# Attention queries and keys in two float32r parts, 59 rows a head, a pair of heads on two row halves

## The chip, the cores and the metric

The kernel runs on one core of a Trainium2 chip. The metric is the time of one execution on the device in microseconds (us). Engines in the profile: PE is TensorE's matrix products, PEld its loads of the stationary operand, DVE VectorE, ACT ScalarE, POOL GpSimd, SP the engine that issues the transfers.

## The reference, cut to what matters

Input x is (1, 2048, 256) in float32. The model is feed-forward, attention, feed-forward, twice. The first pair of feed-forward layers has ternary weights and a silu gate, the second pair keeps 2 of each 4 hidden values. Both attentions are causal with 16 heads of 16:

```python
scores = einsum('bhqd,bhkd->bhqk', q, k) / sqrt(16)
# first attention: + slopes[h] * (k_pos - q_pos) for keys up to the query; second: q and k are rotated (RoPE)
scores = where(key > query, -inf, scores)
attn = softmax(scores, axis=-1)
y = einsum('bhqk,bhkd->bhqd', attn, v)
```

## The kernel before

The order of the phases is setup, feed-forward, qkv, attention, output projection, feed-forward, then the same again for the second layer. Each phase writes out one program per engine, and the engines meet at semaphores.

**qkv_phase** (L631) makes queries, keys and values for four blocks of 512 tokens. Each query or key element is split in three bf16 parts: ScalarE makes the first (L718), VectorE the remainder (L753), ScalarE the second (L706), GpSimd the third (L786). SP stores them to qk_scratch in DRAM (L825) and loads the keys back, head by head, to g.kt (L812): six sections of 16 rows (SROWS = 96, the products of parts in K_PARTS and Q_PARTS), three rows for the maxima, and in the first layer twelve for the ALiBi bias. So a head's contraction has 111 rows in the first layer and 99 in the second, and one head fills the array's rows.

**attention_phase** (L840) goes through 16 steps, one for each query block qb (0 to 3) and group hg of four heads; for qb from 1 the first two groups are a hardware loop (steps, L886). A step has 4(qb+1) key tiles of 128, called units u. In each unit TensorE makes the transposed scores of two pairs of heads (scores, L952, matmul at L964, with a mask product at L962 on the four diagonal units), ScalarE takes the exponential of two heads at once (L1118), and TensorE multiplies with the values of four heads, in float32, on four column tiles (values, L969, L980). These three are the step's places, three to a unit. PSUM banks 0 to 3 hold scores, 4 the output, 5 to 7 the products for the maxima.

The softmax needs each query's maximum before the step begins, so during a step TensorE also makes the products of queries and keys for the next step (max_product, L935, L948), 16(qb+1) items (head, query tile t, key block c), and VectorE reduces each (maxima, L1037): a plain reduction at L1049 for key blocks before the diagonal, a masked one at L1051 for the diagonal block, 128 to 512 wide. Item k uses bank 5 + (k+1) % 3 and waits for item k-3. The items are dealt over the places by max_done (L916); early_items (L913) says how many of the step after next are done at the end of a step. finish_maxima (L1054) negates and splits the maxima in three bf16 parts on VectorE, TensorE transposes them (L987) into bank 5, ScalarE copies them (L1109), and SP writes them as three rows of the queries (rows, L1143, L1146). The next step's scores wait for that transfer (cdma).

The waits on which the order of this work hangs are these:

```python
                if k >= 3:
                    e.wait_ge(s.mx, n + k - 2)            # L945, TensorE, before product k
...
                    if c < qb:
                        e.wait_ge(s.amm, n + k + 1 + (c == qb - 1))   # L1041, VectorE, before item k
```

## Time and profile before

| | us |
|---|---|
| median of the runs | 2012.33 (2009.31 to 2013.27, three runs) |
| profiled execution, span | 2008.3 |
| setup, 0 to 58 | 58 |
| first feed-forward, 58 to 194 | 136 |
| first qkv phase, 194 to 298 | 104 |
| first attention phase, 298 to 804 | 506 |
| first projection and second feed-forward, 804 to 972 | 168 |
| third feed-forward with its weights, 972 to 1162 | 190 |
| second qkv phase, 1162 to 1284 | 122 |
| second attention phase, 1284 to 1795 | 511 |
| second projection and fourth feed-forward, 1795 to 2008 | 213 |

How to read the rows below. A row of the windows has the stretch, its length, the busy time of each engine with the number of its instructions, TensorE's granted clock (1.00 is 2.4 GHz, 0.50 is 1.2 GHz), the share of time in which the DMA engines were busy, and GB/s. The windows of single steps begin and end where ScalarE ends its copy of a step's output (L1125). A row of the timeline has the start, the duration, engine, line, operation, output and inputs, how many instructions were merged, and in brackets how long the engine stood idle before it and who released it. TensorE's instructions overlap, so for them the distance between starts counts, not the duration.

### The profile page before, as it was taken

Reading aid. Unit: us, or ns where it says so; the run is one execution under the profiler, and the core shown is the slowest. Engines: PE = TensorE matmul, PEld = TensorE weight load, DVE = VectorE, ACT = ScalarE, POOL = GpSimd, SP = SyncE. Lnnn points to the kernel's source line nnn. Section 1 sums busy time; section 2 is a strip of 40 time slices with the busy share of each in tenths; the row PEclk is TensorE's granted clock in tenths of the full one; section 3 lists DMA queues with packets and bytes.
Section 4 is the critical chain, followed back from the end, with each engine's and each line's share of the span. In section 5 each row is a group of like instructions: output and inputs, shape, how many; then the busy total and the mean of one; then the engine's idle time right before and its main releaser. Section 6 shows DMA issues by size and latency. Waiting matters only on the chain. (4 is left out here: it accounts for less than half of the span.)

```text
span 2008.3 us, 29496 instructions
## 1 busy us (share of the span) xinstructions
PE 1627.6 (81%) x9772; PEld 913.3 (45%) x9772; DVE 1360.9 (68%) x3268; ACT 913.0 (45%) x1275; POOL 299.6 (15%) x227
## 2 busy tenths in 40 slices
PE   1687717898999999798599587279999999998896
PEld 0576613333333332687488466033333333336786
DVE  8664407778788881565599664277888888713897
ACT  3443404454655668244343222144565566661342
POOL 5332300000000000133043344000000000000243
PEclk9998858999999999899799788599999999998998
DMA  3001892111111000100100048711111110000000
GB/s 114 21 1 20 170 190 47 44 40 42 31 46 31 22 26 12 43 1 0 53 1 0 15 99 178 128 47 33 43 31 37 31 36 22 26 7 1 1 21 22
DMA packets 95600, 86.98 MB, mean 43 GB/s; under 512 B 6255, under 2 KB 92271, under 8 KB 93936
## 3 DMA queue, kind: packets, MB, share of 16 engines
q1 hardware_dynamic: 95490, 85.56, 18.2%
q8 instruction: 64, 1.05, 0.2%
q14 instruction: 46, 0.38, 0.1%
HBM read 62.07 MB, written 23.07 MB: 42 GB/s over the span
## 5 line engine op out<-in xcount | busy, mean ns | idle before, releaser
L1118 ACT ACTIVATE l_att_probs<-psum 128x1024 f32<-128x1024 f32 (+3 forms) x640 | 552.5, 892 | 341.9 <-PE psum L964 337.0
L1049 DVE TENSOR_REDUCE l_att_maxima<-psum 128x1 f32<-128x512 f32 x768 | 511.1, 687 | 140.9 <-PE psum L948 133.6
L948 PE MATMUL psum<-l_kt,l_att_qt 111*128 (+9 forms) x1280 | 416.2, 361 | 130.6 <-DMA l_att_qt<-in_qx_alibi 43.5
L964 PE MATMUL psum<-l_att_qt,l_kt 99*128 (+8 forms) x1280 | 354.1, 352 | 2.2 <-ACT l_att_probs L1118 1.3
L948 PEld LDWEIGHTS psum<-l_kt,l_att_qt 111*128 111x128 bf16 (+3 forms) x1280 | 117.5, 98 | 477.4 <-DVE l_att_maxima L1049 184.1
L980 PE MATMUL psum<-l_att_probs,l_att_vg 128*32 128x512 f32 (+3 forms) x2560 | 303.1, 546 | 5.7 <-ACT l_att_probs L1118 5.0
L1051 DVE CUSTOM_DVE_ANT_0 l_att_junk<-psum,consts 128x128 bf16<-128x128 f32 (+3 forms) x512 | 245.5, 481 | 0.0
L132 POOL TENSOR_TENSOR rstd<-var,mhalf 128x4 f32<-128x4 f32 x24 | 24.3, 1011 | 1285.8 <-DVE var L111 1285.8
L964 PEld LDWEIGHTS psum<-l_att_qt,l_kt 111*128 111x128 bf16 (+3 forms) x1280 | 118.4, 99 | 123.0 <-ACT l_att_probs L1118 37.5
L962 PE MATMUL psum<-later,identb 128*128 128x128 bf16 x512 | 105.3, 225 | 6.4 <-DMA l_att_qt<-l_att_ct 5.5
L980 PEld LDWEIGHTS psum<-l_att_probs,l_att_vg 128*32 128x32 f32 x2560 | 51.0, 108 | 98.0 <-issue 66.9
L1044 DVE COPY fence<-mhalf 128x1 f32<-128x1 f32 x128 | 19.2, 150 | 90.8 <-PE psum L948 90.5
L679 PE MATMUL psum<-l_qkv_xh,l_wqkv_h 128*128 128x512 f32 x96 | 46.5, 484 | 29.4 <-DVE l_qkv_xl L152 22.6
L1109 ACT ACTIVATE l_att_ct<-psum 12x512 bf16<-12x512 bf16 x32 | 18.5, 579 | 102.4 <-PE psum L987 102.1
L573 POOL TENSOR_TENSOR ffn1a_hl<-ffn1a_abs,ffn1a_hh 128x512 fp32r<-128x512 f32 x32 | 51.7, 1644 | 84.6 <-ACT ffn1a_hh L431 84.6
L573 POOL TENSOR_TENSOR ffn1b_hl<-ffn1b_abs,ffn1b_hh 128x512 fp32r<-128x512 f32 x32 | 51.7, 1644 | 84.6 <-ACT ffn1b_hh L431 84.6
L1076 DVE RECIPROCAL l_att_rinv<-psum 128x16 f32<-128x16 f32 x32 | 8.0, 251 | 80.8 <-PE psum L994 80.8
L962 PEld LDWEIGHTS psum<-later,identb 128*128 128x128 bf16 x512 | 50.4, 100 | 24.4 <-DMA l_att_qt<-l_att_ct 7.8
L354 PE MATMUL psum<-ffn0a_xh,w_ternary 128*128 128x512 f32 x128 | 53.5, 418 | 9.2 <-DVE ffn0a_h L478 7.8
L354 PE MATMUL psum<-ffn0b_xh,w_ternary 128*128 128x512 f32 x128 | 52.9, 413 | 9.2 <-DVE ffn0b_h L478 7.8
L354 PE MATMUL psum<-ffn1b_xh,wgu_h 128*128 128x512 f32 x128 | 51.3, 401 | 3.9 <-DVE ffn1b_xl L152 2.8
L354 PE MATMUL psum<-ffn1a_xh,wgu_h 128*128 128x512 f32 x128 | 51.3, 401 | 3.9 <-DVE ffn1a_xl L152 2.8
(200 smaller groups left out, 2998.4 us busy)
## 6 DMA issues: line engine op xcount, KB each, us to landing
l_att_vg<-v_scratch SPq DMA_DIRECT2D x80, 256.0 KB, 2.9
qk_scratch<-l_qkv_parts SPq DMA_DIRECT2D x32, 384.0 KB, 11.3
l_kt<-qk_scratch SPq DMA_DIRECT2D x48, 256.0 KB, 9.8
l_att_qt<-qk_scratch SPq DMA_DIRECT2D x156, 64.0 KB, 2.5
v_scratch<-l_qkv_vst SPq DMA_DIRECT2D x8, 1024.0 KB, 13.1
l_att_qt<-qk_scratch SPq DMA_DIRECT2D x12, 192.0 KB, 6.5
set_raw<-in_w_gu SPq DMA_DIRECT2D x2, 1024.0 KB, 6.5
x_resident<-in_x SPq DMA_DIRECT2D x1, 2048.0 KB, 15.5
```

The lines of the kernel that those rows point to most:

```text
L132: e.tensor_tensor(g.rstd[:, :], g.var[:, :], g.mhalf[:, :], ALU.pow).then_inc(s.rstd, 1)
L354: ins = e.matmul(g.ps[:, slots[c] + half, :], w_up[w][:, k, col:col + P], xp[x][:, k, :], start=k == 0 and q == 0, stop=k == KD - 1 and q ...
L573: e.tensor_tensor(hl[:, c // GCH, c % GCH, :], hs[:, c // GCH, c % GCH, :], hh[:, c // GCH, c % GCH, :].bitcast(F32), ALU.subtract).then_i ...
L679: ins = e.matmul(g.ps[:, bank, :], wq[w][:, k, col:col + P], xp[x][:, k, :], start=k == 0 and q == 0, stop=k == KD - 1 and q == len(terms) ...
L948: e.matmul(g.ps[:, 5 + (k + 1) % 3, 0:w], qt[:, ds(hg * HG + h, 1), t * P:(t + 1) * P].rearrange("p a t -> p (a t)"), g.kt[0:krows, ds(hg ...
L962: e.matmul(g.ps[:, h, off:off + P], g.identb[:, :], g.later[:, :], start=True, stop=False, skip_group_check=True)
L964: ins = e.matmul(g.ps[:, h, off:BLK], g.kt[0:krows, ds(hg * HG + h, 1), kt * P:(kt + 1) * P].rearrange("p a t -> p (a t)"), qt[:, ds(hg * ...
L980: ins = e.matmul(g.ps[h * VW:(h + 1) * VW, 4, off:BLK], vg[:, kt, h * VW:(h + 1) * VW], pr[:, u % 2, h, off:BLK], start=u == 0, stop=qb == ...
L1044: e.tensor_copy(g.fence[:, k % 4:k % 4 + 1], g.mhalf[:, 0:1])
L1049: e.tensor_reduce(dst, src, AX.X, ALU.max).then_inc(s.mx, 1)
L1051: e.tensor_tensor_reduce(out=junk[:, t, 0:w], in0=src, in1=mask[:, BLK - w:BLK], scale=1.0, scalar=NEG, op0=ALU.add, op1=ALU.max, accum_ou ...
L1118: e.activation(pr[:, u % 2, 2 * pair:2 * pair + 2, off:BLK], g.ps[:, 2 * pair:2 * pair + 2, off:BLK], ACT.Exp, scale=HD ** -0.5).then_inc( ...
```

## The change

Queries and keys are split in two float32r parts in place of three bf16 parts: ScalarE makes the first, VectorE the second, and GpSimd and ScalarE make no third and second part. Three sections of 16 rows remain; with three rows for the maxima and eight for the bias a head has 59 rows in the first layer and 51 in the second. Even heads lie in partitions 0 to 63, odd heads in 64 to 127 of the same tile (kt, qt: 8 pairs in place of 16 heads), so both are loaded by two transfers a section, and the row transfer of the maxima becomes two. The scratch in DRAM is float32. The mask product of 128 rows becomes two of 64 rows for each head. Products for the maxima come in pairs of heads, and the items, their shares (early_items, max_done, max_early) and both waits go by pairs. On VectorE the odd item of the block before the diagonal waits for the two diagonal products behind it, and for qb = 0 one wait and one fence stand before each pair. The loops over blocks and groups are written out. Setup copies the bias tables from DRAM to DRAM. The slots for the parts in the qkv phase are three, not four.

```diff
-SROWS = 6 * HD
-Q_PARTS = (0, 0, 1, 0, 2, 1)
-K_PARTS = (0, 1, 0, 2, 0, 1)
+NPAIR = HEADS // 2
+HALF = P // 2
+Q_PARTS = (0, 0, 1)
+K_PARTS = (0, 1, 0)
+SECS = len(Q_PARTS)
+XROW = 2 * HD
+MROWS = 3
...
+            for to, of in [("kx", "in_kx"), ("qx_alibi", "in_qx_alibi"), ("qx_rope", "in_qx_rope")]:
+                e.dma_start(a[to], a[of]).then_inc(s.xin, 16)
+            e.wait_ge(s.xin, 80)
...
-        parts = sb("parts", [P, NM, 3, BLK], BF16)
+        NS = 3
+        parts = sb("parts", [P, NS, 2, BLK], F32R)
...
-            def second_part(b, m):
-                e.wait_ge(s.r1, b * NM + m + 1)
-                e.activation(parts[:, m, 1, :], z[:, m, :], ACT.Copy).then_inc(s.p1, 1)
...
+                    if b * NM + m >= NS:
+                        e.wait_ge(cp[slot(b, m)], stored(b, m) - 16)
...
-            def third_part(b, m):
-                e.wait_ge(s.p1, b * NM + m + 1)
-                e.tensor_tensor(parts[:, m, 2, :], z[:, m, :], parts[:, m, 1, :], ALU.subtract).then_inc(s.p2, 1)
...
+                for sec in range(SECS):
+                    src = a["qk_scratch"][K_PARTS[sec], 1, :, ds(b * BLK, BLK)].rearrange("(h r d) t -> r d h t", r=2, d=HD)
+                    for r in range(2):
+                        row = r * HALF + section(sec)
+                        e.dma_start(g.kt[row:row + HD, :, ds(b * BLK, BLK)].bitcast(F32), src[r]).then_inc(s.kl, 16)
...
-        qt = sb("qt", [krows, HEADS, BLK], BF16)
+        mrow = XROW + g.bias_rows
+        qt = sb("qt", [P, NPAIR, BLK], F32R)
...
+        def steps(body):
+            order = [(qb, hg) for qb in range(NB) for hg in range(NG)] + [(None, 0), (None, 1)]
+            for st in range(NB * NG):
+                body(*order[st], *order[st + 1], *order[st + 2])
+
+        def rows_of(h):
+
+            return slice(h % 2 * HALF, h % 2 * HALF + krows)
...
-            return 0 if qb is None else HG * TPB * (qb + 1) // 5
+            return 0 if qb is None else HG * TPB * (qb + 1) // 10 * 2
...
-            return min(n, early + -(-(n - early) * at // (row_place(qb) - (4 if qb else 2))))
+            return min(n, early + 2 * -(-(n - early) // 2 * at // (row_place(qb) - (4 if qb else 2))))
...
-            return [(h, t, c) for h in range(HG) for t in range(TPB) for c in range(qb + 1)]
+            return [(2 * p + r, t, c) for p in range(HG // 2) for t in range(TPB) for c in range(qb + 1) for r in range(2)]
...
-                if k >= 3:
-                    e.wait_ge(s.mx, n + k - 2)
+                if k >= 2 and k % 2 == 0:
+                    e.wait_ge(s.mx, n + k - 1)
                 w = BLK if c < qb else (t + 1) * P
-                e.matmul(g.ps[:, 5 + (k + 1) % 3, 0:w], qt[:, ds(hg * HG + h, 1), t * P:(t + 1) * P].rearrange("p a t -> p (a t)"),
-                         g.kt[0:krows, ds(hg * HG + h, 1), c * BLK:c * BLK + w].rearrange("p a t -> p (a t)"),
-                         start=True, stop=True).then_inc(s.amm, 1)
+                pair = (hg * HG + h) // 2
+                e.matmul(g.ps[:, 5 + (k + 1) % 3, 0:w], qt[rows_of(h), pair, t * P:(t + 1) * P],
+                         g.kt[rows_of(h), pair, c * BLK:c * BLK + w], start=True, stop=True).then_inc(s.amm, 1)
...
                 if u == 0 and pair == 0:
-                    e.wait_ge(s.cdma, 16 * (step(qb, hg) + 1))
+                    e.wait_ge(s.cdma, 32 * (step(qb, hg) + 1))
                 if not (qb == 0 and isinstance(hg, int) and hg == 0 and u == 0):
                     e.wait_ge(s.ex, 2 * un - 1 + pair)
+                if u < TPB:
+                    for c in range(2):
+                        for x in range(2):
+                            half = slice(x * HALF, (x + 1) * HALF)
+                            e.matmul(g.ps[:, 2 * pair + x, off:off + P], g.tri[half, c * P:(c + 1) * P],
+                                     g.tri[half, (2 + c) * P:(3 + c) * P], start=c == 0, stop=False, skip_group_check=True)
                 for x in range(2):
-                    h = 2 * pair + x
-                    if u < TPB:
-                        e.matmul(g.ps[:, h, off:off + P], g.identb[:, :], g.later[:, :], start=True, stop=False,
-                                 skip_group_check=True)
-                    ins = e.matmul(g.ps[:, h, off:BLK], g.kt[0:krows, ds(hg * HG + h, 1), kt * P:(kt + 1) * P].rearrange("p a t -> p (a t)"),
-                                   qt[:, ds(hg * HG + h, 1), off:BLK].rearrange("p a t -> p (a t)"),
-                                   start=u >= TPB, stop=True, skip_group_check=u < TPB)
+                    hp = hg * HG // 2 + pair
+                    ins = e.matmul(g.ps[:, 2 * pair + x, off:BLK], g.kt[rows_of(x), hp, kt * P:(kt + 1) * P],
+                                   qt[rows_of(x), hp, off:BLK], start=u >= TPB, stop=True, skip_group_check=u < TPB)
                 ins.then_inc(s.st, 1)
...
-                        e.wait_ge(s.amm, n + k + 1 + (c == qb - 1))
-                    elif qb == 0:
-                        e.wait_ge(s.amm, n + k + 1)
-                        e.tensor_copy(g.fence[:, k % 4:k % 4 + 1], g.mhalf[:, 0:1])
+                        e.wait_ge(s.amm, n + k + (3 if c == qb - 1 and k % 2 else 1))
+                    elif qb == 0 and k % 2 == 0:
+                        e.wait_ge(s.amm, n + k + 2)
+                        e.tensor_copy(g.fence[:, k // 2 % 4:k // 2 % 4 + 1], g.mhalf[:, 0:1])
...
-                e.dma_start(qt[SROWS:SROWS + 3, ds(hg * HG, HG), :], ctt[:, :]).then_inc(s.cdma, 16)
+                for r in range(2):
+                    e.dma_start(qt[r * HALF + mrow:r * HALF + mrow + MROWS, hg * HG // 2:(hg + 1) * HG // 2, :].bitcast(F32),
+                                ctt[r * MROWS * HG // 2:(r + 1) * MROWS * HG // 2, :].bitcast(F32)).then_inc(s.cdma, 16)
...
-        g.cst = sb("consts", [P, 3 * P + BLK], F32)
+        g.cst = sb("consts", [P, 2 * P + BLK], F32)
+        g.tri = sb("tri", [P, 4 * P], BF16)
...
-                    g.kt = sb(f"{name}_kt", [g.krows, HEADS, TOK], BF16, c2)
+                    g.kt = sb(f"{name}_kt", [P, NPAIR, TOK], F32R, c2)
...
-    a["qk_scratch"] = nc.dram_tensor("qk_scratch", (3, 2, D, TOK), BF16, kind="Internal").ap()
+    a["qk_scratch"] = nc.dram_tensor("qk_scratch", (2, 2, D, TOK), F32, kind="Internal").ap()
+    for n in ("kx", "qx_alibi", "qx_rope"):
+        a[n] = nc.dram_tensor(n, arrays[f"in_{n}"].shape, F32, kind="Internal").ap()
```

## Rows read from the trace of the kernel before

**Rows 1.** Page, busy times of the engines over the span.
```profile
PE 1627.6 (81%) x9772; PEld 913.3 (45%) x9772; DVE 1360.9 (68%) x3268; ACT 913.0 (45%) x1275; POOL 299.6 (15%) x227
```

**Rows 2.** Windows, one per step: length, busy PE, PEld, DVE, ACT, POOL, clock, DMA.
```profile
325.37:337.96 12.59, 9.81 (x88) 4.78 (x88) 9.55 (x55) 6.37 (x10) 0.00 (x0) 1.00 0.21 59
...
351.06:374.59 23.53, 17.01 (x104) 6.21 (x102) 18.97 (x56) 6.69 (x10) 0.00 (x0) 0.93 0.15 43
...
400.51:425.55 25.04, 23.12 (x154) 8.44 (x154) 18.80 (x55) 14.51 (x20) 0.00 (x0) 1.00 0.14 40
...
450.61:482.13 31.52, 28.12 (x170) 9.55 (x168) 27.91 (x72) 14.62 (x18) 0.00 (x0) 1.00 0.11 32
482.13:517.85 35.72, 33.70 (x218) 12.03 (x216) 28.66 (x72) 22.16 (x26) 0.00 (x0) 1.00 0.15 44
...
589.49:632.05 42.56, 39.15 (x234) 12.89 (x232) 37.97 (x88) 22.38 (x26) 0.00 (x0) 1.00 0.11 31
...
679.08:725.97 46.89, 45.41 (x282) 15.27 (x280) 38.85 (x88) 30.12 (x34) 0.00 (x0) 1.00 0.08 23
725.97:770.45 44.48, 42.89 (x271) 13.86 (x270) 32.70 (x75) 30.09 (x34) 0.00 (x0) 1.00 0.09 25
770.45:803.90 33.45, 31.04 (x208) 7.53 (x205) 0.68 (x2) 28.95 (x33) 0.00 (x0) 1.00 0.03 9
```

**Rows 3.** Timeline inside step (3,1), first stage: start, us, engine, line, idle before.
```profile
701.30 0.69 DVE L1049 TENSOR_REDUCE l_att_maxima<-psum 128x1 f32<-128x512 f32 x1 [0.86 <-PE psum L948]
...
702.04 0.10 PEld L948 LDWEIGHTS psum<-l_kt,l_att_qt 111*128 x1 [0.63 <-DVE l_att_maxima L1049]
...
702.38 1.88 DVE L1049 TENSOR_REDUCE l_att_maxima<-psum 128x1 f32<-128x512 f32 x3
...
703.44 1.06 PE L980 MATMUL psum<-l_att_probs,l_att_vg 128*32 128x512 f32 x8
...
704.44 0.39 PE L948 MATMUL psum<-l_kt,l_att_qt 111*128 x1
...
704.87 2.04 DVE L1049 TENSOR_REDUCE l_att_maxima<-psum 128x1 f32<-128x512 f32 x3
```

**Rows 4.** Timeline, float32r products after a standstill, second qkv stage, PE and PEld.
```profile
1213.71 0.50 PE L679 MATMUL psum<-l_qkv_xh,l_wqkv_h 128*128 128x512 f32 x1 [2.37 <-DVE y L748]
...
1213.82 0.19 PEld L679 LDWEIGHTS psum<-l_qkv_xl,l_wqkv_h 128*128 128x128 f32 x1
...
1214.04 0.39 PE L679 MATMUL psum<-l_qkv_xl,l_wqkv_h 128*128 128x512 f32 x1
1214.27 0.40 PE L679 MATMUL psum<-l_qkv_xh,l_wqkv_l 128*128 128x512 f32 x1
```

**Rows 5.** Groups by shape on DVE, first attention stage: widest and narrowest diagonal items.
```profile
L1051 DVE CUSTOM_DVE_ANT_0 l_att_junk<-psum,consts 128x512 bf16<-128x512 f32 x64 | 43.6, 681 | 0.0
...
L1051 DVE CUSTOM_DVE_ANT_0 l_att_junk<-psum,consts 128x128 bf16<-128x128 f32 x64 | 18.0, 281 | 0.0
```

**Rows 6.** Timeline, a product of 128 columns and the item it releases.
```profile
335.54 0.22 PE L948 MATMUL psum<-l_kt,l_att_qt 111*128 111x128 bf16 x1
...
335.79 0.15 DVE L1044 COPY fence<-mhalf 128x1 f32<-128x1 f32 x1 [0.88 <-PE psum L948]
```

**Rows 7.** Timeline, end of step (0,1): last finishing operation, row transfer, next step.
```profile
334.69 0.23 DVE L1070 TENSOR_TENSOR l_att_crow<-l_att_crem,l_att_crow 128x16 bf16<-128x16 f32 x1
...
336.01 0.72 SPq L1146 DMA_DIRECT2D l_att_qt<-l_att_ct  x1
...
338.21 0.10 PEld L962 LDWEIGHTS psum<-later,identb 128*128 128x128 bf16 x1 [1.19 <-DMA l_att_qt<-l_att_ct]
```

**Rows 8.** Page, a costly group and a DMA issue.
```profile
L1049 DVE TENSOR_REDUCE l_att_maxima<-psum 128x1 f32<-128x512 f32 x768 | 511.1, 687 | 140.9 <-PE psum L948 133.6
...
qk_scratch<-l_qkv_parts SPq DMA_DIRECT2D x32, 384.0 KB, 11.3
```

**Rows 9.** DMA view of 194 to 300 us in 40 slices: GB/s moved.
```profile
GB/s 0 0 0 0 112 151 148 281 297 102 177 110 112 114 111 205 376 374 148 165 140 173 269 386 313 207 127 125 129 210 406 306 159 118 120 123 48 104 147 167
```

More of the change, by code:

```diff
@@ L732, in _ @@
             act_hi(e, g, s, 0)
-            blocks_of(e, body)
+            for b in range(NB):
+                body(b)
         @block.vector
@@ L776, in _ @@
             dve_lo(e, g, s, 0)
-            blocks_of(e, body)
+            for b in range(NB):
+                body(b)
         @block.gpsimd
@@ L831, in _ @@
             load_k(NB - 1)
-            e.wait_ge(s.kl, 96 * NB)
+            e.wait_ge(s.kl, 16 * 2 * SECS * NB)
             e.wait_ge(s.vd, 16 * NB)
-            e.wait_ge(s.vtab, 16)
-            for c in range(NM):
-                e.wait_ge(cp[c], 16 * NB)
+            e.wait_ge(s.vtab, 32)
+            for n in range(NM * NB - NS, NM * NB):
+                e.wait_ge(cp[slot(n // NM, n % NM)], stored(n // NM, n % NM))
 def attention_phase(nc, g, name, a, qx):
@@ L1096, in _ @@
             maxima(0, 1, 0, early_items(0))
-            steps(e, body)
+            steps(body)
             normalise(NG * NB)
@@ L1127, in _ @@
             rows(0, 0)
-            steps(e, body)
+            steps(body)
         @block.sync
@@ L1327, in shape_constants @@
     groups = (q // GROUP == k // GROUP).astype(f32)
-    consts = np.concatenate([ident, mask, groups, np.where(q > k, f32(NEG), f32(0)).astype(f32)], axis=1)
+    consts = np.concatenate([ident, mask, groups], axis=1)
+    later = np.where(q > k, f32(NEG), f32(0)).astype(f32)
+    tri = np.concatenate([np.concatenate([m[c * HALF:(c + 1) * HALF]] * 2, axis=0) for m in (ident, later) for c in range(2)], axis=1)
     slope = (f32(4) * f32(2) ** (f32(-8) / np.arange(1, HEADS + 1, dtype=f32))).astype(f32)
-    parts, rest = [], slope
-    for _ in range(3):
-        p = rest.astype(bf)
-        parts.append(p)
-        rest = rest - p.astype(f32)
-    pos = np.arange(TOK)
-    high, low = (pos // P * P).astype(f32), (pos % P).astype(f32)
-    kx = np.zeros((15, HEADS, TOK), f32)
-    qx = np.zeros((15, HEADS, TOK), f32)
-    kx[0:3] = 1
-    for n, p in enumerate(parts):
-        p = p.astype(f32)[:, None]
-        r = 3 + 4 * n
-        kx[r], qx[r] = high, p
-        kx[r + 1], qx[r + 1] = p, -high
-        kx[r + 2], qx[r + 2] = low, p
-        kx[r + 3], qx[r + 3] = p, -low
+    high = (slope.view(np.uint32) & np.uint32(0xFFFFF000)).view(f32)
+    pos = np.arange(TOK)
+    places = (pos // P * P).astype(f32), (pos % P).astype(f32)
+    kx = np.zeros((8 + MROWS, HEADS, TOK), f32)
+    qx = np.zeros((8 + MROWS, HEADS, TOK), f32)
+    kx[8:] = 1
+    for n, p in enumerate([high, slope - high]):
+        for m, place in enumerate(places):
+            r = 4 * n + 2 * m
+            kx[r], qx[r] = place, p[:, None]
+            kx[r + 1], qx[r + 1] = p[:, None], -place
     theta = np.power(f32(10000.0), np.repeat(-np.arange(0, HD, 2, dtype=f32) / f32(HD), 2)).astype(f32)
```

122 lines of the change are left out of this document (55 added, 67 removed).

## The prediction

> **What bounds the kernel now.** I read three views in this order. The page's busy times come first [rows 1]: TensorE is busy 81% of the span, VectorE 68%. That is an average over stages, so the second view cuts one attention stage into its steps, one window for each [rows 2]. A step is one (query block qb, group of four heads); the reader should compare the PE column with the length. From qb = 1 on TensorE is busy 89 to 97% of a step; VectorE is busy 74 to 89% (not in the last step, which has no maxima), ScalarE less until then. The third view is the timeline of the middle of a qb = 3 step [rows 3]. TensorE does eight products of 512 columns and the four heads' values in one unit of some 2.7 us. The values hold it for 1.00 us (703.44 to the product at 704.44), eight products at 0.21 us take 1.7 us, and nothing is left. So the qb = 3 steps are bounded by TensorE, but closely: VectorE is busy 38.85 of 46.89 us. The two attention stages are 506 and 511 us of the span of 2008.3 us (table of stages); the feed-forward stages aren't touched.
>
> **What the edit does to TensorE.** Each head's 111 or 99 rows become 59 or 51 in one half of the partitions, so a pair of heads can run together. The trace of before has no row halves. It has four column tiles (the values, eight instructions in 1.06 us [rows 3], each in float32). Taken singly, a product today takes 0.21 us; a pair of float32r products costs between one stream of 0.23 us (start to start, 1214.04 to 1214.27 [rows 4]) and two, 0.46 us. I take 0.25, since the column tiles do overlap. A unit then needs 4 x 0.25 + 1.00 = 2.0 us of TensorE in place of 2.7. The Trainium skill (TensorE: Matmul & The Clock Gate, Part 3, The mechanism) says that products on different row groups start within a few ns of each other; by it the pair would be 0.24. If that were all, qb = 3 steps would fall to what VectorE needs.
>
> **VectorE's chain, which is what the edit tightens.** The three banks 5 to 7 hold the products whose maxima VectorE takes. Before, product k waits only for item k-3, so VectorE has up to two finished products in hand while TensorE fetches the next. After, a pair k, k+1 (k even) waits for item k-2, the first of the pair before. When VectorE ends that item it has one product in hand. Worse, the odd item of the last off-diagonal key block (c = qb-1) now waits for the whole diagonal pair behind it (amm n+k+3), and that pair is released only by the item just ended. There VectorE stands still for one full round trip, once for each (pair of heads, query tile): eight times a step.
>
> The round trip from rows: item end to TensorE's start 0.05 (701.30 + 0.69 to 702.04), the product's start to VectorE's start 0.43 (704.44 to 704.87) [rows 3]: 0.48 for bf16. A float32r product that starts from a standstill shows 0.50 in place of 0.39, because its weights take 0.11 first (1213.71 to the next load at 1213.82) [rows 4]. So R1 = 0.59 for the first product, and R2 = 0.70 where both are waited for, with 0.11 for the second's weights. For 128 columns the handoff is 0.25 (335.54 to 335.79 [rows 6]) in place of 0.43, so R2 = 0.52; mean over the four diagonal widths 0.62. Bounds: 0.48 (weights of both hidden) and 0.92 (the two products in series, 0.22 more).
>
> VectorE's own work: a reduction every 0.60 us ((1.88 - 0.69) / 2 [rows 3]), though it ends 0.69 after its start; diagonal items 0.61, 0.48, 0.34, 0.21, i.e. 0.07 under their durations of 0.68 to 0.28 [rows 5], 1.64 for four. The finishing of the maxima and the normalisation are 1.9 us a step (the finish ends with the row at 334.69 [rows 7], 1.3 us after the last maximum, and 0.6 for the normalisation). So a set of 16(n+1) items for next block n costs 9.6n + 6.6 us.
>
> Stalls per group of one query tile: from one pair of reductions to the next 0.69 + 0.59 - 1.19 = 0.09, which occurs n-1 times; before the odd item 0.69 + 0.62 - 0.60 = 0.71; after the diagonal pair (duration + 0.59 - twice the spacing) 0.45, 0.32, 0.18, 0.05, mean 0.25. That is 0.96, 1.05, 1.14 for n = 1, 2, 3, and with eight groups sets of 23.9, 34.2 and 44.5 us (0.75, 0.71, 0.70 an item) in place of 16.2, 25.8 and 35.4.
>
> This holds only while TensorE already stands at its wait when VectorE releases it. A pair holds TensorE 0.40 us; in a qb = 3 step 26 pairs are dealt over 37 places, so that each values of 1.00 shares its gap with one pair of score products, 0.25: 1.65 us against 1.28 between releases. That is 0.37 late, at 13 of 16 units, and three of four such gaps are tight: 3.4 us a step (bounds 0 and 6). For qb = 2 I take 2.5, for qb = 1 0.8.
>
> **Step by step** (before [rows 2], after = set + 1.9 + lateness; each step reduces its successor's items and the even number of early ones after that; steps not shown are like their neighbours). (0,3): 23.5 to 26.3, +2.8. (1,0) to (1,2): about 25 to 26.6, 26.6 and 27.8 (eight items of the last belong to qb = 2), +5.0. (1,3): 31.5 to 37.1, a full n = 2 set, +5.6. (2,0) to (2,2): about 35.8 to 38.6, 38.6 and 40.9, +10.8. (2,3): 42.6 to 47.8, +5.2. (3,0), (3,1): 46.9 to 49.8, +5.7. (3,2): 44.5 to 46.5, 52 items and then ScalarE's pace, +2.0. (3,3): no maxima; ScalarE, busy 28.95 of 33.45, becomes the bound with 1.5 us of gaps: 30.5, -3.0. Sum +34.1 us.
>
> Steps of qb = 0 (12.59 us): VectorE's maxima, their finish, and the row transfer that the next step waits for form one loop; the transfer's issue at 336.01 and TensorE's restart at 338.21 close it [rows 7]. The fence stands before each pair only (7 x 0.07 us back), but each pair waits for both products: 0.35, 0.27, 0.18 and 0 per four, 1.6 a step; one item fewer is done early, 0.4; TensorE behind a values, 0.8; a second transfer on SP's queue, 0.4 to 0.7 ahead of the loads behind it. Together +3.0 a step, three steps: +9. The first 16 maxima, with nothing beside them and TensorE at half clock, +4. One stage +47.1, two stages +94.
>
> **The rest.** The queries and keys are stored as 512 KB in place of 384, 32 times [rows 8]: 4.2 MB more, at the 400 GB/s at which the stores move in the peaks of [rows 9], 10.5 us. The key and query loads keep their bytes (six halves of float32 for six thirds of bf16), so their plateau of 110 to 120 GB/s [rows 9] stays. A third part on GpSimd and a second on ScalarE go, about 1.9 us ahead of the store, at four of the eight blocks on the path: -7.5. Net +3, bounds -11 and +10. Setup's four extra transfers come last in its queue, 3.3 MB or 28 us at that plateau, beside the rounding of the weights, which fills the 58 us of setup (table of stages): 0, and +5 at most if x came late. Mask products double in number but run in pairs: 0. Loops written out: TensorE's address instructions go; they are hidden, 0. Sum: 2008.3 + 94 + 3 = 2105; the median of the runs lies 4 us above this execution's span, so 2109 us.
>
> The Trainium skill states the same limit in general (TensorEngine Tiling (Array Packing), PSUM Bottleneck): tiling speeds TensorE, not the emptying of PSUM. The trace agrees, VectorE being within 8 us of the step; but by that page alone the steps could only stay or shrink, for the stalls come from the waits.
>
> **Rivals.**
> A, faster: the handoff costs no more than in bf16 (0.48, and 0.50 for both) and TensorE is always parked. For: TensorE has 0.7 us a unit to spare. Against: the 0.11 of [rows 4]. Stalls are then 0.76 a group, the sets 22.3, 31.9, 41.5 us; (3,0) to (3,2) gain 3.6, 3.6, 3.2, (3,3) 3, while (1,3), (2,3) and qb = 0 still lose: -9 a stage, 1997 us. It decides where a group's stall and lateness fall under (46.9 - 37.3) / 8 = 1.2 us at qb = 3, 1.0 at qb = 2 and 0.9 at qb = 1. Chance 0.13.
> B, pairs don't run together: the products come in series or a change of shape between values, mask and products empties the array. Then R2 grows by 0.11 (8 groups, 13 steps: 11 us a stage) and each unit's tight gap by some 0.35, at 130 of 160 units (46 us); with qb = 0, +60 a stage: 2229 us. Against: the column tiles. The Trainium skill (TensorEngine Tiling, Key Properties) says that a change of tiling mode drains the array; the values' own 1.00 us already holds such a change. Chance 0.13.
> C, the chain as computed, but TensorE never late (-22 a stage) and the round trip 0.05 shorter (three handoffs, 8 groups, 26 steps, -31): 2109 - 44 - 31 = 2034 us. Chance 0.12.
> The forecast has 0.62, with its own range 2055 to 2170 (lateness none, or twice).
>
> **How the numbers follow.** The range reaches over C and into A below and to B's foot above: 2005 to 2210 leaves out most of A (0.12) and part of B (0.08). A measurement of this kernel tells 0.2%, 4 us, from no change. Faster: A, 0.13. Same: the edge between A and C, 0.03. Slower: 0.84.
>
> **What would show it.** In the after trace: VectorE's wait for the product ahead of its reductions rises from 133.6 us [rows 8] to 250 or more, with single waits of 0.6 to 0.8 us eight times a step; TensorE's busy share in qb = 3 steps falls to about 75%; the lengths of (1,3) and (2,3) grow most, (3,3) shrinks to about 30.5. Two products of a pair start within 0.15 us of one another; if 0.2 or more, B. It is wrong if VectorE's reductions run on at 0.6 us through the odd item, or if qb = 3 steps fall under 45 us.

## The result and the profile after

The changed kernel takes 2258.0 us (median of four runs, 2253.1 to 2263.6) against 2010.8 us (2009.1 to 2013.3): ratio 1.122, 95% interval 1.120 to 1.125. The profiled execution has a span of 2251.2 us against 2008.3 us, so there are 242.9 us to place. Line numbers have moved: L948 is now L952, L964 is L970, L980 is L985, L1049 is L1054, L1051 is L1056, L1125 is L1131.

Two rows of the page of after, the engines' busy times (answering [rows 1]) and the clock in 40 slices, and its row for the reductions and the DMA issue (answering [rows 8]):

```profile
PE 1706.6 (76%) x10284; PEld 982.2 (44%) x10284; DVE 1373.2 (61%) x3203; ACT 895.3 (40%) x1243; POOL 261.3 (12%) x195
...
PEclk9997756676787998899799785557587677889998
...
L1054 DVE TENSOR_REDUCE l_att_maxima<-psum 128x1 f32<-128x512 f32 x768 | 512.1, 688 | 337.4 <-PE psum L952 332.1
...
qk_scratch<-l_qkv_parts SPq DMA_DIRECT2D x32, 512.0 KB, 11.3
```

The same window per step as in [rows 2]; these are (0,1), (0,3), (1,1), (1,3), (2,0), (2,3), (3,0) to (3,3). The number to compare besides the length is the granted clock, the third from the end:

```profile
333.49:349.25 15.76, 12.22 (x104) 6.18 (x104) 9.27 (x47) 6.54 (x11) 0.00 (x0) 0.72 0.19 50
...
368.75:400.11 31.36, 22.05 (x124) 9.90 (x120) 19.09 (x55) 6.77 (x10) 0.00 (x0) 0.50 0.13 34
...
433.53:466.79 33.26, 27.13 (x174) 10.99 (x170) 19.19 (x55) 14.36 (x19) 0.00 (x0) 0.64 0.12 33
...
499.50:544.32 44.82, 33.17 (x190) 13.37 (x190) 29.51 (x71) 14.44 (x19) 0.00 (x0) 0.62 0.08 24
544.32:589.59 45.27, 37.58 (x239) 13.75 (x236) 29.39 (x71) 22.06 (x27) 0.00 (x0) 0.74 0.12 35
...
677.86:732.11 54.25, 40.81 (x254) 14.97 (x254) 39.69 (x87) 22.63 (x28) 0.00 (x0) 0.78 0.09 25
732.11:782.71 50.60, 40.47 (x302) 14.98 (x301) 39.69 (x87) 30.28 (x35) 0.00 (x0) 0.97 0.13 37
782.71:834.66 51.95, 42.01 (x304) 15.08 (x301) 39.66 (x87) 30.27 (x35) 0.00 (x0) 0.93 0.07 22
834.66:885.07 50.41, 42.50 (x290) 15.23 (x285) 32.71 (x73) 30.05 (x35) 0.00 (x0) 0.86 0.08 22
885.07:916.91 31.84, 28.38 (x218) 8.90 (x216) 0.68 (x2) 28.25 (x33) 0.00 (x0) 1.00 0.03 9
```

From the end of the first step to the end of the last, the first attention stage takes 583.4 us (478.5 before) at a clock of 0.79 (1.00 before), the second 604.6 (481.2) at 0.72 (0.98). That is 228.3 of the 242.9 us. The rest is 8.1 us up to the end of the first step, 5.2 between the stages and 1.3 behind them. The steps that grow by a quarter or more, (0,1) to (2,0) and (2,3) in the first stage, have clocks of 0.50 to 0.78; (3,0) and (3,1), at 0.97 and 0.93, grow by 8 and 11%. Before, every step shown ran at 0.93 or more.

Timeline of after at full clock, in (3,0): a pair of products, the values behind it, and the odd item that waits.

```profile
744.92 0.50 PE L952 MATMUL psum<-l_kt,l_att_qt 59*128 59x512 f32 x2 [0.55 <-DVE l_att_maxima L1054]
...
745.49 0.69 DVE L1054 TENSOR_REDUCE l_att_maxima<-psum 128x1 f32<-128x512 f32 x1 [0.63 <-PE psum L952]
```

And at half clock, in (2,3): values, then two pairs.

```profile
702.04 1.93 PE L985 MATMUL psum<-l_att_probs,l_att_vg 128*32 128x512 f32 x8
...
703.90 0.58 PE L952 MATMUL psum<-l_kt,l_att_qt 59*128 59x256 f32 x2
...
704.56 0.69 DVE L1054 TENSOR_REDUCE l_att_maxima<-psum 128x1 f32<-128x512 f32 x1 [1.72 <-PE psum L952]
...
705.64 0.80 PE L952 MATMUL psum<-l_kt,l_att_qt 59*128 59x512 f32 x2 [0.73 <-DVE l_att_maxima L1056]
```

At full clock VectorE stands 0.63 us before this odd item. The item before it lasts 0.69, so from start to start it is 1.32 us, 0.72 more than the 0.60 of reductions in a row; the prediction had 0.71 as the mean over the widths of the diagonal. At half clock one set of values holds TensorE 1.86 us (702.04 to 703.90) in place of 1.00, and the wait ahead of the next reduction is 1.72 us.

### The profile page after: what moved, and what is told of

Read it like the earlier page. It is cut to its first block and busy times, and to the rows that moved or that the text cites. A ratio compares the mean times of both kernels' runs of the same rounds, so it can differ in the third digit from the quotient of the medians.

```text
span 2251.2 us, 27578 instructions
## 1 busy us (share of the span) xinstructions
PE 1706.6 (76%) x10284; PEld 982.2 (44%) x10284; DVE 1373.2 (61%) x3203; ACT 895.3 (40%) x1243; POOL 261.3 (12%) x195
## 5 line engine op out<-in xcount | busy, mean ns | idle before, releaser
L1054 DVE TENSOR_REDUCE l_att_maxima<-psum 128x1 f32<-128x512 f32 x768 | 512.1, 688 | 337.4 <-PE psum L952 332.1
L952 PE MATMUL psum<-l_kt,l_att_qt 59*128 59x512 f32 (+7 forms) x1280 | 366.6, 569 | 283.3 <-DVE l_att_maxima L1056 105.6
L952 PEld LDWEIGHTS psum<-l_kt,l_att_qt 59*128 59x128 f32 (+1 forms) x1280 | 153.5, 236 | 602.1 <-DVE l_att_maxima L1054 263.0
L985 PE MATMUL psum<-l_att_probs,l_att_vg 128*32 128x512 f32 (+3 forms) x2560 | 381.6, 679 | 4.7 <-ACT l_att_probs L1124 3.5
L970 PE MATMUL psum<-l_att_qt,l_kt 51*128 51x512 f32 (+6 forms) x1280 | 311.1, 501 | 4.6 <-ACT l_att_probs L1124 4.5
L1056 DVE CUSTOM_DVE_ANT_0 l_att_junk<-psum,consts 128x128 bf16<-128x128 f32 (+3 forms) x512 | 228.3, 483 | 0.0
L970 PEld LDWEIGHTS psum<-l_att_qt,l_kt 59*128 59x128 f32 (+1 forms) x1280 | 153.2, 239 | 87.7 <-ACT l_att_probs L1124 45.2
L985 PEld LDWEIGHTS psum<-l_att_probs,l_att_vg 128*32 128x32 f32 x2560 | 56.2, 120 | 103.7 <-issue 51.2
L966 PE MATMUL psum<-tri 64*128 64x128 bf16 x1024 | 87.5, 258 | 12.1 <-DMA l_att_qt<-l_att_ct 11.0
L1049 DVE COPY fence<-mhalf 128x1 f32<-128x1 f32 x64 | 9.8, 153 | 122.7 <-PE psum L952 122.4
L966 PEld LDWEIGHTS psum<-tri 64*128 64x128 bf16 x1024 | 34.3, 110 | 83.6 <-issue 57.0
L1115 ACT ACTIVATE l_att_ct<-psum 12x512 fp32r<-12x512 bf16 x32 | 18.8, 586 | 115.6 <-PE psum L992 115.3
L360 PE MATMUL psum<-ffn1b_xh,wgu_h 128*128 128x512 f32 x128 | 51.3, 401 | 3.9 <-DVE ffn1b_xl L156 2.8
## 6 DMA issues: line engine op xcount, KB each, us to landing
qk_scratch<-l_qkv_parts SPq DMA_DIRECT2D x32, 512.0 KB, 11.3
```

What stands on the lines that cost most here:

```text
L360: ins = e.matmul(g.ps[:, slots[c] + half, :], w_up[w][:, k, col:col + P], xp[x][:, k, :], start=k == 0 and q == 0, stop=k == KD - 1 and q ...
L952: e.matmul(g.ps[:, 5 + (k + 1) % 3, 0:w], qt[rows_of(h), pair, t * P:(t + 1) * P], g.kt[rows_of(h), pair, c * BLK:c * BLK + w], start=True ...
L966: e.matmul(g.ps[:, 2 * pair + x, off:off + P], g.tri[half, c * P:(c + 1) * P], g.tri[half, (2 + c) * P:(3 + c) * P], start=c == 0, stop=Fa ...
L970: ins = e.matmul(g.ps[:, 2 * pair + x, off:BLK], g.kt[rows_of(x), hp, kt * P:(kt + 1) * P], qt[rows_of(x), hp, off:BLK], start=u >= TPB, s ...
L985: ins = e.matmul(g.ps[h * VW:(h + 1) * VW, 4, off:BLK], vg[:, kt, h * VW:(h + 1) * VW], pr[:, u % 2, h, off:BLK], start=u == 0, stop=qb == ...
L1054: e.tensor_reduce(dst, src, AX.X, ALU.max).then_inc(s.mx, 1)
```

## The experiments

Two things changed together: the hand-off of the maxima (order of items, two waits) and the operands (half rows, float32r). Theory 1: the hand-off alone lengthens the steps. Theory 2: it also takes TensorE's clock down. Theory 3: the light half-row work takes the clock down, whatever the waits. First I undid the waits, then I put the waits on the old operands, then I varied the operands under equal waits. "Attention" below is the two stages, first step's end to last step's end, with their clocks.

| kernel | us (ratio to before, interval) | attention | clock |
|---|---|---|---|
| before | 2011 to 2015 | 478.5, 481.2 | 1.00, 0.98 |
| after | 2258 (1.120 to 1.125) | 583.4, 604.6 | 0.79, 0.72 |
| a1_single | 2219 (1.097 to 1.106) | 572.7, 588.3 | 0.77, 0.72 |
| a2_fence | 2129 (1.055 to 1.064) | 513.3, 542.1 | 0.86, 0.78 |
| a3_both | 2070 (1.022 to 1.037) | 495.1, 516.2 | 0.89, 0.81 |
| a4_old_order | 2177 (1.078 to 1.082) | 534.2, 579.7 | 0.83, 0.73 |
| a5_fill | 2338 (1.156 to 1.166) | 624.8, 652.7 | 0.84, 0.79 |
| a7_keep | 2491 (no interval) | 695.6, 743.9 | 0.75, 0.68 |
| a8_dup | 2180 (1.079 to 1.089) | 545.2, 557.6 | 0.96, 0.93 |
| a9_fullrows | 2133 (1.057 to 1.063) | 517.0, 515.0 | 0.99, 0.99 |
| b1_pairs | 2166 (1.074 to 1.079) | 549.0, 552.0 | 0.96, 0.94 |
| b2_order | 2011 (0.998 to 1.000) | 475.3, 475.6 | 0.99, 0.99 |
| b3_rows65 | 2120 (1.046 to 1.059) | 521.3, 516.5 | 0.85, 0.86 |
| b4_mix | 1995 (0.989 to 0.993) | 470.2, 470.3 | 1.00, 1.00 |

The runs of a7_keep lie between 2415 and 2525 us, too far apart for an interval; the profiled one took 2513. The clocks and stages are those of each kernel's profiled execution.

**The two waits, undone.** a2_fence changes VectorE's side; a1_single TensorE's; a3_both has both edits.

```diff
-                    if c < qb:
-                        e.wait_ge(s.amm, n + k + (3 if c == qb - 1 and k % 2 else 1))
-                    elif qb == 0 and k % 2 == 0:
+                    if c < qb:
+                        e.wait_ge(s.amm, n + k + 1)
+                    elif k % 2 == 0:
...
-                if k >= 2 and k % 2 == 0:
-                    e.wait_ge(s.mx, n + k - 1)
+                if k >= 3:
+                    e.wait_ge(s.mx, n + k - 2)
```

Expected of a2_fence: 

> After, with one change: the odd item ahead of the diagonal no longer waits for the two diagonal products; these get a wait and a fence of their own, as qb = 0 has. TensorE's wait by pairs stays. Theory 1 (the hand-off alone lengthens the steps): the standstill of 0.71 us before the odd item goes, eight times a step, to about 0.1; 24 steps with such items, so some 5 us each, -115 us: about 2145, and the clock in attention stays near 0.77. Theory 2 (TensorE's standstills also take its clock down): the same -115 and part of the clock back, above 0.85: 2060 to 2120. Theory 3 (the clock falls since half-row products count as little work, whatever the waits): clock lower or equal, as the same work is pressed into less time only slightly: 2145 to 2180.

Expected of a1_single (run last): 

> After, with TensorE's wait by pairs undone alone: product k waits for item k-3 again; VectorE's odd item still waits for both diagonal products. Known by now: without the odd wait 2129, without either 2070 us, after 2258. By the prediction's own stalls the odd wait costs 0.71 us a group and stays, while 0.09 between pairs of reductions and 0.25 after the diagonal pair go, 8 groups in 26 steps: 50 to 70 us less, 2190 to 2210, if the two waits add up. If they are one loop (VectorE stands at the odd wait until the second diagonal product has come, whose release is the item just ended in either form), much less goes: 2220 to 2250.

Expected of a3_both: 

> After, with both waits relaxed: TensorE's product k waits for item k-3 only, as before the change, and the diagonal products have a wait and fence of their own. Order of items, row halves and formats stay. Theory 1 (hand-off alone): all stalls of the sets go but the hand-off of the diagonal's second product; sets near 16, 26 and 36 us; at the clock of the present after (0.77 in attention) TensorE's half-clock stretches remain: 2080 to 2130. Theory 2 (clock follows the standstills): steps of qb = 3 near 40 us, clock at 0.95, 1930 to 1990, faster than before. Theory 3 (clock falls with half rows): clock stays 0.77 or lower, 2080 to 2150, steps of qb = 3 alternating between 40 and 60 us of pace.

a2_fence gives 129 us back, a1_single 39, both 188. Together they give 20 us more than the sum, but that is no more than the intervals of the four kernels leave open, so it isn't shown that the two waits are one loop. a1_single lies at the foot of its second expectation. In a3_both (3,0) and (3,1) run at full clock and are 1.4 to 1.5 us shorter than before, but (0,1) and (1,3) stay slow at a low clock. Windows of a3_both, (0,1), (1,3), (3,0):

```profile
331.96:349.28 17.32, 14.57 (x104) 8.21 (x104) 9.29 (x47) 6.74 (x10) 0.00 (x0) 0.60 0.15 46
...
469.47:505.67 36.20, 32.94 (x192) 15.14 (x189) 28.67 (x79) 14.47 (x19) 0.00 (x0) 0.76 0.11 29
...
659.72:705.24 45.52, 41.91 (x302) 17.30 (x302) 38.94 (x95) 29.93 (x36) 0.00 (x0) 1.00 0.14 41
```

So the waits move the clock in part, from 0.79 and 0.72 to 0.89 and 0.81 in the two stages. But theory 2, by which it comes back to 0.95 with them (1930 to 1990 us), is wrong; something else holds it down too. In one respect a3_both isn't the same work: where each product waits by itself, more than half of the neighbouring products for the maxima start 0.2 us or more apart, so many pairs no longer run together.

**The waits on the old operands.** b1_pairs is the kernel before with after's order, shares and both waits; b2_order has the same order with a3_both's waits.

Expected of b1_pairs: 

> Before, with its three bf16 parts and full rows, but with the order of items by pairs of heads, their shares of places, TensorE's wait by pairs, and VectorE's wait of the odd item for the diagonal pair, all as after. Work is unchanged. Theory 1 (hand-off): eight standstills a step of 0.7 to 0.8 us appear in kernels that have no row halves, and TensorE, 95% busy, cannot make them up: +4 to +8 us a step for 26 steps, 2110 to 2230. Theory 2: the clock also falls in attention, from 0.98 to under 0.9. Theory 3 (half rows lower the clock): clock stays at 0.95 or more. A rival by which the waits cost nothing gives 2010 to 2030.

Expected of b2_order: 

> Before (three bf16 parts, full rows) with the order of items and shares of after, but TensorE's wait for item k-3 and a wait and fence of their own for the diagonal products: the relaxed waits of the 2070-us kernel on the old operands. Against it that kernel shows what the half rows alone do. Theory 3: clock 0.92 or more over the span and 2005 to 2025 us, so that the half rows cost 50 us more than the full ones under the same waits. Rival (the order of items by pairs is what takes the clock): clock near 0.86 and 2050 to 2080 us here too.

b2_order is level with before, so the order costs nothing. b1_pairs against b2_order, the paired waits alone on full rows, is 155 us; after against a3_both, the same waits on half rows, is 188 us. b1_pairs, (1,3), (2,0), (3,0):

```profile
480.39:524.83 44.44, 36.24 (x169) 11.09 (x168) 29.20 (x71) 14.63 (x18) 0.00 (x0) 0.73 0.08 23
524.83:565.44 40.61, 34.19 (x218) 11.61 (x217) 29.19 (x71) 22.27 (x26) 0.00 (x0) 1.00 0.14 39
...
695.25:746.58 51.33, 46.22 (x282) 15.18 (x281) 39.41 (x87) 30.24 (x34) 0.00 (x0) 1.00 0.12 36
```

(2,0) and (3,0) show the waits at full clock: 40.6 and 51.3 us. (1,3), a short step with a long set of maxima, fell to 0.73 even with full rows.

**What holds the clock down.** The cleanest test is b3_rows65. It is b2_order with the contraction of products and scores cut to 65 rows; a9_fullrows is a3_both with both halves' rows in every product.

```diff
# b3_rows65, in both products
-qt[:, ds(hg * HG + h, 1), ...]   g.kt[0:krows, ds(hg * HG + h, 1), ...]
+qt[0:65, ds(hg * HG + h, 1), ...]   g.kt[0:65, ds(hg * HG + h, 1), ...]
# a9_fullrows, in rows_of
-            return slice(h % 2 * HALF, h % 2 * HALF + krows)
+            return slice(0, HALF + krows)
```

Expected of b3_rows65: 

> The kernel with bf16 parts, full rows and relaxed waits (2011 us), with the contraction of the products for the maxima and of the scores cut from 111 and 99 rows to 65 (the other parts, the bias and the maxima rows are left out of the sums, so its output is not the reference's). Every instruction, wait, column and load stays; only the rows that TensorE works on are as few as a half-row product's. Rival R (few rows lower the clock): the qb = 0 steps go to a clock of 0.5 to 0.7 and 17 to 20 us, the span's clock under 0.88, 2050 to 2070 us. Rival D (the float32r form and the row tiling, not the number of rows): clock and time stay, 0.92 or more and 2005 to 2020 us.

Expected of a9_fullrows: 

> The 2070-us kernel (after with relaxed waits) with each product for the maxima and each score product over partitions 0 to 122, both heads' rows at once, in place of one half (the sums then hold two heads, so its output is not the reference's; the five unused rows are set to zero, which adds two memsets, one of them ahead of the first key loads, some 10 to 15 us a layer). Float32r stays, but no product runs on a row half, and none beside another. Rival R (few rows lower the clock): full rows, so the clock returns to 0.92 or more, and the attention steps are those of the bf16 kernel with the same waits, 475 us from the first step's end to the last one's, plus what the exposed float32r weights cost (0.11 us for some 40 products a step that wait for VectorE: up to 20 us a stage). Rival F (float32r itself lowers the clock): clock at 0.5 to 0.7 in qb = 0 and 490 us or more for the stage, whatever the rows. Rival T (switching between row halves and column tiles drains the array, and that takes the clock): as R for the clock, and the mean hold of a pair ahead of the values falls to two streams, 0.45.

Windows of b2_order, (0,1), (1,3), (3,0):

```profile
326.90:340.92 14.02, 10.10 (x88) 4.67 (x88) 9.27 (x47) 6.47 (x10) 0.00 (x0) 1.00 0.18 53
...
453.19:485.89 32.70, 27.99 (x169) 9.51 (x168) 28.35 (x79) 14.60 (x18) 0.00 (x0) 1.00 0.12 31
...
632.75:679.05 46.30, 45.38 (x282) 15.23 (x281) 39.05 (x95) 29.93 (x35) 0.00 (x0) 1.00 0.14 40
```

The same steps of b3_rows65:

```profile
331.37:349.44 18.07, 17.01 (x89) 7.72 (x88) 9.28 (x47) 6.76 (x10) 0.00 (x0) 0.50 0.16 41
...
478.34:521.26 42.92, 41.26 (x168) 12.14 (x167) 28.79 (x79) 14.85 (x18) 0.00 (x0) 0.60 0.08 24
...
683.24:729.53 46.29, 45.33 (x282) 15.18 (x281) 39.02 (x95) 29.91 (x34) 0.00 (x0) 1.00 0.14 40
```

And of a9_fullrows:

```profile
352.96:368.59 15.63, 12.69 (x104) 7.22 (x104) 9.26 (x47) 6.82 (x10) 0.00 (x0) 1.00 0.19 51
...
491.40:525.95 34.55, 32.68 (x185) 16.06 (x185) 28.64 (x79) 14.70 (x18) 0.00 (x0) 1.00 0.12 31
...
684.69:735.15 50.46, 50.41 (x297) 25.70 (x297) 39.40 (x95) 30.26 (x34) 0.00 (x0) 1.00 0.13 37
```

b3_rows65 has the format, instructions, columns and waits of b2_order and no row halves. Where its clock is 1.00 its steps are those of b2_order ((3,0): 46.29 and 46.30); where it isn't, (0,1) takes 18.07 us at 0.50 and (1,3) 42.92 at 0.60. It costs some 100 us (runs of 2104, 2108, 2132 and 2137 against 2009 to 2018), more than the range I gave. So fewer rows at work are enough to take the clock down, without float32r and without row halves. Which steps fall varies: (2,2) has 0.74 in the first stage and 1.00 in the second, (2,3) the other way round. With fewer rows the sums, and so the values, differ too; no run changed the values alone. a9_fullrows has float32r, and with all rows its clock is 1.00 in these steps, so float32r by itself doesn't take it down. But its products run one by one, so TensorE is also busier, and a share of the row halves themselves isn't excluded. What a9_fullrows loses is TensorE's time (busy 50.41 of 50.46 us at (3,0)); its first step also ends 26 us later than that of b2_order, with the zeroing of the unused rows ahead of it.

**More work for TensorE.** a8_dup issues the half-row products twice; a5_fill (on after) and a7_keep (on a3_both) add full-row products with a zero stationary operand.

```diff
# a8_dup; the score products alike
+                for twice in range(2):
-                e.matmul(g.ps[:, 5 + (k + 1) % 3, 0:w], ...).then_inc(s.amm, 1)
+                    ins = e.matmul(g.ps[:, 5 + (k + 1) % 3, 0:w], ...)
+                ins.then_inc(s.amm, 1)
# a7_keep, ahead of the wait for item k-3; a5_fill: two of 512 columns behind the values
+                    e.matmul(g.ps[:, 4, 0:BLK // 2], zero[:, :], g.tri[:, 0:BLK // 2], start=False, stop=False, ...)
```

Expected of a8_dup: 

> The kernel with both waits relaxed (2070 us), every product for the maxima and every score product of units past the diagonal issued twice, the second overwriting the first: it computes the same. Work of the half-row kind is doubled, so TensorE is as full as in the kernel before. Theory 3 by idle time: clock at 0.95 or more in all steps with qb from 1, and better than 0.8 at qb = 0; qb = 3 steps 46 to 50 us by TensorE; 2030 to 2090, no dearer than the kernel without the copies. Theory 3 by form (float32r or half rows count little): clock stays at or under 0.8 in the qb = 0 and (x,3) steps, and since a half-clock stretch now holds twice the work, 2150 or more.

Expected of a5_fill: 

> After, with work added and none removed: behind each unit's values (qb from 1, not the last unit) two products of a zero stationary operand with 512 columns of bf16, accumulated to the output's bank, 0.21 us each at full clock: 264 units, 528 products, 111 us more of TensorE's time. Nothing waits for them but the products behind. Theory 1 (hand-off alone): TensorE has room, but is later at its waits: 2258 to 2330, never less. Theory 2 and 3 (the clock falls because TensorE does too little): clock of the attention stretch rises from 0.77 above 0.88, and the time falls in spite of the added work, to 2120 to 2200.

Expected of a7_keep: 

> The kernel with both waits relaxed (2070 us), with a filler ahead of each wait of a product for the maxima (from the step's fifth place on): a product with a zero stationary operand, 256 columns of bf16, accumulated to the output's bank. It stands where TensorE would mostly wait anyway. Theory 3 (clock falls since TensorE has too little to do while it waits): the clock of the steps (0,1) to (1,0) rises over 0.8, (1,3) and (2,3) to 0.95; 1980 to 2030. If the clock follows something else than the work in hand (the standstills' number or length, or the float32r form), it stays where it was and the time grows by 10 to 40 us.

a8_dup: the first stage has 0.98 or more in every step from (1,0); (0,1) to (0,3) have 0.70 or 0.71. The second has 1.00 in most, but 0.83 in (1,0) and (1,3), and 0.56 to 0.69 in (0,1) to (0,3). So more work of the same half-row kind brings the clock back in most steps, though the copies cost more than it returns ((3,0) is 53.8 us, TensorE busy 53.3). The fillers gave no time back, and those of a7_keep did the opposite of what I expected: its stages have clocks of 0.75 and 0.68, a3_both's 0.89 and 0.81. a7_keep, its window of (3,0), two stretches of 3 us in it, and its timeline at full clock and, in the same step, at half clock:

```profile
749.89:832.85 82.96, 81.88 (x348) 29.92 (x348) 41.20 (x95) 30.40 (x35) 0.00 (x0) 0.65 0.08 22
...
767.00:770.00 3.00, 3.00 (x10) 1.19 (x8) 1.65 (x4) 1.34 (x2) 0.00 (x0) 0.50 0.31 87
...
818.00:821.00 3.00, 3.00 (x14) 0.68 (x13) 2.10 (x9) 1.02 (x1) 0.00 (x0) 0.50 0.00 0
```
```profile
753.80 0.28 PE L950 MATMUL psum<-tri,l_att_zero 128*128 128x256 bf16 x1
754.02 0.50 PE L955 MATMUL psum<-l_kt,l_att_qt 59*128 59x512 f32 x1
754.45 0.28 PE L950 MATMUL psum<-tri,l_att_zero 128*128 128x256 bf16 x1
...
793.83 0.79 PE L955 MATMUL psum<-l_kt,l_att_qt 59*128 59x512 f32 x1
794.56 0.39 PE L950 MATMUL psum<-tri,l_att_zero 128*128 128x256 bf16 x1
```

A half-row product between two full-row ones takes 0.43 us at full clock (754.02 to 754.45) where a full-row float32r product takes 0.23 [rows 4]. Filler and product together take 0.65 us (753.80 to 754.45) for 768 columns, which at the pace of [rows 4] would take 0.34, and the pair no longer runs together. The Trainium skill (TensorEngine Tiling (Array Packing), Key Properties) says that a change of tiling mode drains the array. The trace is in keeping with it: the two changes and the weights that stand ahead of each product cost 0.31 us together. So TensorE was busy 81.88 of 82.96 us, and its clock was 0.65; from 767 to 821 us it was busy without a gap, by its records, and had half the clock throughout. The busy share alone doesn't tell the clock: b3_rows65's (1,3) is another case, busy 41.26 of 42.92 at 0.60. Whether the zeros count in that, I did not try. a5_fill keeps pairs together. In the first stage it raised the clock of (2,0) from 0.74 to 0.96, but not that of (1,0) (0.65 in both); over the stages it went from 0.79 and 0.72 to 0.84 and 0.79, at 80 us more in all.

**Old order on half rows.** a4_old_order keeps the half rows but deals the items as before, so a product for the maxima has no partner.

```diff
-            return [(2 * p + r, t, c) for p in range(HG // 2) for t in range(TPB) for c in range(qb + 1) for r in range(2)]
+            return [(h, t, c) for h in range(HG) for t in range(TPB) for c in range(qb + 1)]
```

Expected of a4_old_order: 

> After, but the items for the maxima in the old order (head, query tile, key block), with the old shares of places, TensorE's wait for item k-3 and VectorE's old wait (one product more at the last block before the diagonal). Only the operands stay as after: float32r, half rows; score products still run in pairs. Theory 2 (the standstills of the paired waits took the clock): clock in attention back to 0.95 or more, 1980 to 2010. Theory 3 (the light half-row work itself lets the clock fall wherever VectorE sets the pace): clock of the qb = 0 steps stays at 0.5 to 0.7, (1,3) and (2,3) under 0.9, and the time stays at 2050 to 2090 in spite of the old waits.

2177 us, 107 more than a3_both and beyond what either theory gave. Windows of (0,1), (3,0) and (3,1):

```profile
332.12:349.36 17.24, 17.03 (x107) 9.30 (x104) 10.12 (x55) 6.77 (x11) 0.00 (x0) 0.50 0.16 46
...
686.32:742.34 56.02, 54.50 (x298) 23.77 (x296) 39.03 (x88) 30.25 (x34) 0.00 (x0) 0.79 0.12 33
742.34:789.47 47.13, 44.62 (x298) 19.95 (x296) 38.49 (x88) 30.14 (x34) 0.00 (x0) 1.00 0.08 24
```

The same work takes 56.0 us in (3,0) and 47.1 in (3,1). A reading of this, not tested by a run, is that the low clock keeps itself going: at half clock TensorE is the bound (busy 54.5), and it gets through few rows a microsecond. It does end, though, with TensorE as busy as before.

**A better kernel.** Against before, b2_order is up to 1.7 us shorter in most steps from (0,3) on (the expectation below puts that too high), but 1.2 us longer in (1,3), and 1.4 and 3.5 us in (0,1) and (0,2), in the first stage. b4_mix takes the pair order with relaxed waits for qb from 1 and the old order for qb = 0, on bf16 and full rows.

```diff
+            if qb == 0:
+                return [(h, t, 0) for h in range(HG) for t in range(TPB)]
             return [(2 * p + r, t, c) for p in range(HG // 2) for t in range(TPB) for c in range(qb + 1) for r in range(2)]
```

Expected of b4_mix: 

> A candidate to beat both: bf16 parts and full rows as before; for qb from 1 the items by pairs of heads with relaxed waits and a fence (in the 2011-us kernel these steps were 0.5 to 2.5 us shorter each than before), for qb = 0 the old order, shares and waits (where the order by pairs cost 1.4 and 3.5 us in two steps). If the two parts are independent: 2012 less 4 to 8 us a stage for the steps from (0,3), less nothing at qb = 0: 1992 to 2002 us, ratio 0.990 to 0.995. If the gain from (0,3) on was borrowed from a later start of the step: 2005 to 2015.

1995 us, 0.9911 of before (0.9889 to 0.9932): faster than both. Every step of both stages has a clock of 1.00; (0,1) is back at 12.6 us. (0,3) takes 20.6 in both stages, where before it took 23.5 at 0.93 and 26.2 at 0.69: 8.6 of the 19 us that the two stages gain lie in this one step, and part of them is clock.

## Why the prediction was wrong in size

The sign was right, and 2258 us lies above the range of 2005 to 2210.

- **The chain of hand-offs: right, as far as full clock shows it.** The one step of after near full clock is (3,0): 50.6 us at 0.97 (49.8 forecast), with waits of 0.45 to 0.63 us before most of its odd items (0.6 to 0.8 forecast). b1_pairs, on the old operands and at full clock, has 40.6 and 51.3 us in (2,0) and (3,0) where 38.6 and 49.8 were forecast for the new ones. VectorE's wait rose from 133.6 [rows 8] to 332.1 us (250 or more forecast), the low clock included; b1_pairs has 252.9. TensorE's busy share in (3,0) to (3,2) is 80 to 84%, not 75%.
- **The step that failed: "One stage +47.1", worked out at full clock throughout.** I read the clock in [rows 2], 1.00 in nearly every step, and took it as given. The second stage, whose steps I took to be like the first's, had a warning: before, its (0,3) ran at 0.69 and took 26.2 us, the first's 23.5 at 0.93. Of the 47.1, 40.1 lie behind the first step; measured there are +104.9 and +123.4 us. The sum has no term for the clock, although the change makes TensorE's work lighter and its waits longer, both at once. b3_rows65 prices the first alone at some 100 us in a kernel without the waits (2120 against 2011). In the changed kernel the half-row form costs 59 us with relaxed waits (2070 - 2011) and 92 with paired ones (2258 - 2166); the waits cost 155 without it and 188 with it. By which order one counts changes the shares, not the sum of 247.
- **qb = 0 and (0,3).** Forecast +3.0 a step and +2.8. (0,1) grew by 3.2, (0,2) by 6.4 (13.1 to 19.5), (0,3) by 7.8, at clocks of 0.72, 0.68 and 0.50. In the second stage all three have 0.50 and grew by 5.2, 6.9 and 5.2. For the first 16 maxima I did price half clock; a few lines later I did not.
- **A pair at 0.25 us: too low, but of little effect at full clock.** Timeline of a3_both at full clock, in (3,1), and one pair ahead of the values in (3,0):

```profile
723.47 0.50 PE L952 MATMUL psum<-l_kt,l_att_qt 59*128 59x512 f32 x2
723.81 0.62 PE L970 MATMUL psum<-l_att_qt,l_kt 59*128 59x512 f32 x4
724.27 0.97 PE L952 MATMUL psum<-l_kt,l_att_qt 59*128 59x512 f32 x2
```
```profile
703.09 0.49 PE L952 MATMUL psum<-l_kt,l_att_qt 59*128 59x512 f32 x2
703.51 1.06 PE L985 MATMUL psum<-l_att_probs,l_att_vg 128*32 128x512 f32 x8
```

  The pair at 723.47, behind the values, takes 0.34 us to the next start; the two pairs behind it take 0.46, 0.23 each; ahead of the values a pair takes 0.42. At full clock (3,0) came out within 0.8 us of the forecast all the same. At half clock the pairs of L952 take 0.6 to 0.7.
- **(3,3).** 31.8 us in place of 30.5, against 33.45 before.
- **Rival B's price was near (2229), by luck.** It wanted 0.2 us or more between the starts of a pair. In the changed kernel the two products of every pair of 512 columns start within 0.02 us of one another: the pair at 744.92 lasts 0.50 us, as long as one product alone does at 754.02 in a7_keep. B's other condition, that a change of shape holds TensorE up, is true in part (0.42 ahead of the values against 0.23 in a run of pairs), but a3_both has the same changes and its (3,0) at full clock is shorter than before.
- **Outside these steps: right.** Up to the end of the first step 8.1 us were added, between the stages and in the second stage's first step 5.2, behind them 1.3: 14.6 in all. The forecast had 3 for the qkv phases and, in each stage, 4 for the first 16 maxima and 3 for the first step: 17. The stores of 512 KB land in 11.3 us, as those of 384 KB did [rows 8].

What stays open: why the second stage is the slower one with half rows. In all eight kernels with half rows it takes 12 to 48 us longer than the first, in the others under 5. It has 51 rows a head, the first 59, which agrees with the cause found, but no run changed that number alone. Nor did a run split the 92 us of the half rows under paired waits into clock and pair holds, or change the values of the operands without their rows.

## What to carry to other kernels

When an edit makes an engine's work lighter or its waits longer, put a line for its clock into the sum, beside the chain; full clock in the profile of before is a property of that load, not of the kernel. Packing two small products onto row halves relieves TensorE alone: at full clock it took 3.5 us off its busy time in (3,0) and 0.8 off the step (a3_both against b2_order). And where two engines hand buffers over, coarsening the hand-off from one to two of three buffers takes the slack away; a wait for both diagonal products with a small fence instruction, ahead of the first of their own two items, kept the pair order at no cost here (b2_order).
